# Cross-attention on one core: whole-batch stacks in three buffers, fewer transfers, one exponential per pair of heads

## The chip, the core and the metric

One core of a Trainium2 chip. The metric is the device time of one execution in microseconds; the profile shows one such execution, with the work of TensorE (PE, its weight loads PEld), VectorE (DVE), ScalarE (ACT), GpSimd (POOL) and the transfers, which nearly all are issued by SyncE's queue (SP).

## The reference

Sixteen batches of 256 queries of width 320 attend to 256 keys with 20 heads of 16. The last 8 keys of each batch are special: 4 "dummy" and 4 "ip" keys, which have a softmax of their own and a mask from bounding boxes.

```python
B, S, D = hidden_states.shape                      # 16, 256, 320
text = encoder_hidden_states[:, :end_pos]          # 248 keys of width 512
ip_h = encoder_hidden_states[:, end_pos:]          # 8 keys
q = _split_heads(hidden_states @ w_q, 20)
k, v = _split_heads(text @ w_k, 20), _split_heads(text @ w_v, 20)
out_text = _merge_heads(_sdpa(q, k, v))            # softmax(q k' / 4) v
mask_ip = _ip_mask(bbox, B, S, dtype)
k_ip, v_ip = _split_heads(ip_h @ w_k_ip, 20), _split_heads(ip_h @ w_v_ip, 20)
out_ip = _merge_heads(_sdpa(q, k_ip, v_ip, mask=mask_ip))
out = (out_text + out_ip) @ w_out + b_out + hidden_states
```

## The kernel before

Two stages follow each other; each engine has one instruction stream, written out by hand, with semaphores between them.

**Projections.** Eight groups of two batches (`group(g)` on each engine). PE forms ten tiles: three of K, four of V, three of Q. A float32 product is made of three matmuls with operands split in a high and a low part. ACT copies the high part of a K or Q tile out of PSUM, DVE forms the low part (L533), and SP stores both (L204, L209) in `q_parts` and `k_parts` in DRAM; V goes to `v_rows` (L242). Each part of a buffer is written again only when its store has landed. In the last group the query scores and maxima of batch 0 are interleaved (`FIRST_SCORES`), and SP issues the first stack loads there (`first_loads`).

**Batches.** Every batch has ten pairs of heads. For each of the two heads of a pair a *stack* of rows is built in SBUF: three groups of 16 rows (high, low, high of Q against high, high, low of K), five mask rows, and two rows that carry the negated row maxima. One matmul over 55 rows then gives a score that is already masked and has its maximum taken off. `q_stack` and `k_stack` have two buffers (batch parity `u`), and each is loaded in two halves of five pairs: `load_stack_q` is 6 transfers of parts (L286) and 2 of masks (L289), `load_stack_k` is 6 (L300).

In batch b the engines do, per pair p:
- PE: `key_scores(b, p)` (L728, keys in partitions, into `score_t`), which waits for both exponentials of the pair before it, and at p = 0 and 5 for the rows of maxima of that half; in even pairs `values` of two finished pairs (L745 into `pv`); `query_scores(b + 1, p)` (L675, into `score_q`, 53 rows, which at p = 0 and 5 waits for the stack of the next batch and always for the maxima of two pairs before); in odd pairs `project_out` for batch b - 1 (L755 into `pj`).
- ACT: two exponentials of 512 columns (L477) and, in even pairs, the evacuation of `pv` (L468), behind the exponentials of that pair.
- DVE: `maxima(b + 1, p)` (L542 and L544); in odd pairs `invert` (L598 transposes 32 x 32 blocks, L601 takes reciprocals); `turn_back` (L606) at p = 8 for its own batch and at p = 2 and 4 for the one before, which waits for POOL's sums; `finish` (L613, adds the residual) at p = 0 and 6; at p = 4 and 9 `turn` (L552), which turns the maxima of a half into rows.
- POOL, `normalise(b)`: waits for the residual x of the batch, adds the bias to it (L386), then for each of five blocks scales (L392) and adds (L397).
- SP, `batch(b, u)`: rows of half 1 of b stored (`store_rows`, four transfers, L214), Q half 1 of b + 1, rows of half 1 loaded (`load_rows`, L222, which waits for the store to land), K half 1 of b + 1, output of b - 2 (L343), residual of b (L309), values of b + 1 (L304, L306), rows of half 0 of b + 1 stored, Q half 0 of b + 2 once half of batch b's key scores are done, rows of half 0 loaded, K half 0 of b + 2.

Batches 0, 1, 14 and 15 are written out, 2 to 13 run in a loop of two batches a turn.

## Time and profile before

| | |
|---|---|
| three runs | 658.9, 652.2, 658.66 us; median 658.66 |
| the profiled run's own time | 657.42 us |
| span of its profile | 655.6 us |
| busy: PE, DVE, ACT, POOL | 523.5, 387.5, 297.8, 125.7 us |
| mean granted TensorE clock | 0.911 |
| moved by DMA | 107.36 MB, 164 GB/s over the span |

A span is the time from the first to the last instruction. Engines run side by side, so busy times don't add up, and an engine's idle time costs something only where the work behind it sets the end. A line of the timeline gives start, length, engine and source line, operation, output and inputs, and in brackets how long the engine was idle before it and what ended that. Neighbouring instructions of a kind are merged (x4).

### The profile page before, as it was taken

The numbers are of one execution on the slowest core, as the hardware profiler recorded it, in microseconds if no ns is written. First come the engines' busy times: TensorE is split into PE (matmuls) and PEld (weight loads), VectorE is DVE, ScalarE is ACT, GpSimd is POOL, SyncE is SP. The second block draws the span as 40 slices with busy tenths as digits, with TensorE's granted clock in tenths as the row PEclk, the third lists the DMA queues.
The fourth block names the chain that finished last, engine by engine and source line by source line (L and its number), as shares of the span: only waits on it lengthen the run. The fifth ranks groups of instructions, "written<-read, shape, count | busy, mean of one in ns | idle before, by whom it ended". The sixth has DMA issues, their size and how long they took to land.

```text
span 655.6 us, 13734 instructions
## 1 busy us (share of the span) xinstructions
PE 523.5 (80%) x4304; PEld 337.8 (52%) x4304; DVE 387.5 (59%) x706; ACT 297.8 (45%) x515; POOL 125.7 (19%) x203
## 2 busy tenths in 40 slices
PE   4969899999977667866878678787787877878686
PEld 3868778887855344433434344343443434434342
DVE  2565443435335476847568576685766857668543
ACT  4442443434411454535446364464644646446372
POOL 4040000000000032121322213222132221322232
PEclk9979899999978587979899798898989979889899
DMA  9987888888786645353453624526445363452411
GB/s 270 289 243 166 296 266 287 266 274 283 253 208 164 148 132 152 79 171 83 143 155 86 181 76 144 162 74 171 103 133 156 86 171 94 135 160 77 129 46 40
DMA packets 96808, 107.36 MB, mean 164 GB/s; under 512 B 20988, under 2 KB 75836, under 8 KB 96784
## 3 DMA queue, kind: packets, MB, share of 16 engines
q1 hardware_dynamic: 96032, 105.99, 55.2%
q0 software_dynamic: 752, 1.07, 1.3%
q8 instruction: 13, 0.21, 0.1%
q14 instruction: 11, 0.09, 0.0%
HBM read 68.85 MB, written 38.17 MB: 163 GB/s over the span
## 4 chain that ended last, share of the span: by engine, by line
PE 38%; SPq 22%; issue 13%; DMA 12%; DVE 10%; POOL 2%; ACT 1%; DVEq 1%; POOLq 0%; ACTq 0%
PE pv L745 9%; DMA k_stack<-k_parts 7%; SPq L286 6%; PE pj L755 5%; SPq L300 5%; SPq L214 5%; PE score_q L675 4%; DVE max_cols L542 3%; PE score_t L728 3%; DMA probs<-in_wv_ip 2%; PE score_t L636 2%; PE score_t L637 2%; PE score_t L638 2%; DMA v_rows<-v_out 2%; SPq L289 2%
## 5 line engine op out<-in xcount | busy, mean ns | idle before, releaser
L542 DVE TENSOR_REDUCE max_cols<-score_q 128x4 fp32r<-128x992 f32 x160 | 189.1, 1182 | 142.3 <-PE score_q L675 140.2
L477 ACT ACTIVATE probs<-score_t 128x512 f32<-128x512 f32 x320 | 173.7, 595 | 161.2 <-PE score_t L728 159.6
L745 PE MATMUL pv<-probs,v_cur 128*32 128x256 f32 x1920 | 140.3, 432 | 0.7 <-ACT probs L477 0.6
L675 PE MATMUL score_q<-k_stack,q_stack 53*128 53x256 f32 x640 | 80.6, 332 | 45.8 <-DMA k_stack<-k_parts 40.0
L728 PE MATMUL score_t<-q_stack,k_stack 55*128 55x256 f32 x640 | 79.3, 328 | 36.9 <-ACT probs L477 20.2
L755 PE MATMUL pj<-wo_sb,o_all 128*128 128x320 f32 x192 | 78.8, 510 | 29.0 <-DVE out_sb L613 18.7
L675 PEld LDWEIGHTS score_q<-k_stack,q_stack 53*128 53x128 f32 x640 | 53.4, 204 | 87.9 <-issue 57.3
L728 PEld LDWEIGHTS score_t<-q_stack,k_stack 55*128 55x128 f32 x640 | 52.5, 200 | 76.9 <-issue 42.2
L745 PEld LDWEIGHTS pv<-probs,v_cur 128*32 128x32 f32 x1920 | 59.6, 121 | 50.2 <-issue 19.5
L386 POOL TENSOR_TENSOR x_all<-x_all,bias_sb 128x640 f32<-128x640 f32 x16 | 24.7, 1544 | 305.1 <-DMA x_all<-in_x 305.1
L392 POOL TENSOR_TENSOR o_turned<-o_turned,inv_cols 128x256 f32<-128x256 f32 x80 | 49.6, 620 | 167.4 <-DVE inv_cols L601 167.4
L468 ACT ACTIVATE o_all<-pv 128x512 f32<-128x512 f32 x80 | 47.9, 598 | 53.9 <-PE pv L745 53.9
L598 DVE STREAM_TRANSPOSE o_turned<-o_all 128x512 f32<-128x512 f32 x80 | 55.9, 698 | 11.2 <-ACT o_all L468 11.2
L755 PEld LDWEIGHTS pj<-wo_sb,o_all 128*128 128x128 f32 x192 | 32.0, 201 | 50.8 <-DVE out_sb L613 22.0
L521 DVE TENSOR_TENSOR c_hl<-o_all,c_hl 128x1024 fp32r<-128x1024 f32 x16 | 19.0, 1223 | 54.2 <-ACT c_hl L411 54.2
L397 POOL TENSOR_TENSOR o_all<-o_turned 128x128 f32<-128x128 f32 x80 | 36.4, 456 | 10.1 <-POOL o_turned L392 6.7
L544 DVE TENSOR_REDUCE max_cols<-score_q 128x4 fp32r<-128x32 f32 x160 | 29.0, 181 | 0.0
L422 ACT ACTIVATE qk_out<-score_t 128x512 fp32r<-128x512 f32 (+1 forms) x24 | 14.0, 593 | 27.7 <-PE score_t L638 16.3
L636 PE MATMUL pj<-c_hl,wk_hl 128*128 128x512 f32 x32 | 14.3, 446 | 11.3 <-DVE c_hl L521 11.3
L533 DVE TENSOR_TENSOR qk_out<-score_t,qk_out 128x512 fp32r<-128x512 f32 (+1 forms) x24 | 15.8, 683 | 11.8 <-ACT qk_out L422 11.8
L601 DVE RECIPROCAL inv_cols<-o_turned 128x16 f32<-128x16 f32 x80 | 20.3, 254 | 2.7
L606 DVE STREAM_TRANSPOSE o_all<-o_all 128x256 f32<-128x256 f32 x48 | 20.7, 431 | 1.0 <-POOL o_all L397 1.0
(128 smaller groups left out, 644.8 us busy)
## 6 DMA issues: line engine op xcount, KB each, us to landing
q_stack<-q_parts SPq DMA_DIRECT2D x192, 80.0 KB
k_stack<-k_parts SPq DMA_DIRECT2D x192, 80.0 KB
v_rows<-v_out SPq DMA_DIRECT2D x32, 320.0 KB, 2.4
v_cur<-v_rows SPq DMA_DIRECT2D x16, 640.0 KB
o_all<-in_ctxT SPq DMA_DIRECT2D x16, 512.0 KB, 5.7
q_parts<-qk_out SPq DMA_DIRECT2D x32, 256.0 KB, 2.4
k_parts<-qk_out SPq DMA_DIRECT2D x32, 248.0 KB, 4.4
x_all<-in_x SPq DMA_DIRECT2D x16, 320.0 KB, 3.3
```

The source lines that it names most:

```text
L214: sp.dma_start(max_rows[h].rearrange("r (t i n) -> i r t n", t=2, i=4)[i], row_buf[32 * i:32 * i + 32, h, :].rearrange("r (t n) -> r t n", ...
L286: sp.dma_start(qv[at:at + DH, :, :], src).then_inc(done, 16)
L392: pool.tensor_tensor(out, out, inv_cols[:, k, :].unsqueeze(2).broadcast_to([P, 2 * S // 32, DH]), ALU.mult).then_inc(scaled, 1)
L397: pool.tensor_tensor(o_norm_t[:, k // 2, :, half:half + DH], out[:, 0:S // 32, :], out[:, S // 32:, :], ALU.add).then_inc(o_added, 1)
L468: nc.scalar.activation(o_raw[:, k, :], pv[:, :], ACT.Copy)\
L477: nc.scalar.activation(probs[:, slot(u, p), 2 * S * e:2 * S * (e + 1)], score_t[:, 512 * e:512 * e + 512], ACT.Exp, scale=SCALE)\
L542: nc.vector.tensor_reduce(out=max_cols[:, h, :, at:at + 2].rearrange("p t e -> p e t"), in_=both[:, :, :, 0:TEXT], op=ALU.max, axis=AX.X, ...
L598: nc.vector.transpose(turned_blocks(k), o_raw[:, k, :].rearrange("p (j n) -> p j n", n=32))\
L675: last = mm(score_bank(first, p, e)[:, t * KEYS:(t + 1) * KEYS], q_cols(u, p, e, PART + MASKS, t * P, P), k_cols(u, p, e, PART + MASKS, 0, ...
L728: last = mm(score_t[:, 512 * e + S * tile:512 * e + S * tile + S], k_cols(u, p, e, PART + MASKS + 2, tile * P, P), q_cols(u, p, e, PART + ...
L745: last = mm(pv[32 * t:32 * t + 32, at:at + S], values_of(u, kind, 4 * k + t), probs[:, slot(u, 2 * k + t // 2), a:a + S], start=kind != 1, ...
L755: last = mm(pj[:, 0:D], o_norm[:, u, c, t * P:t * P + P], wo_sb[:, c, :], start=c == 0, stop=c == OC - 1)
```

## The change

Stacks are loaded whole, two batches ahead, into three buffers in turn (`w`, the batch's number modulo 3; `r` counts a buffer's uses). The third lies in `stack2`, where the split context of the projections (`c_hi`, `c_lo`) lies before. `q_parts` is laid out by head, high then low part, so that 32 rows (high and low) of a head come in one transfer: 6 for Q and masks, 6 for K. Two transfers load the constant mask rows of the third buffer (`load_kaux`). SP's order per batch is new. The rows of maxima of a half are stored in one transfer. ACT has one exponential of 1024 columns per pair, and waits once for key scores. PE does query scores ahead of values. The loop body now holds six batches and turns twice.

```diff
-    q_parts = nc.dram_tensor("q_parts", [2, D, B * S], f32, kind="Internal").ap()
+    q_parts = nc.dram_tensor("q_parts", [H, 2, DH, B * S], f32, kind="Internal").ap()
...
+        stack2 = sb("stack2", [P, PAIRS * (S + KEYS)], f32r)
+        c_hi = stack2[:, 0:CC * GT].rearrange("p (c n) -> p c n", c=CC)
+        c_lo = stack2[:, CC * GT:2 * CC * GT].rearrange("p (c n) -> p c n", c=CC)
+        q_stacks = [q_stack[:, 0, :], q_stack[:, 1, :], stack2[:, 0:PAIRS * S]]
+        k_stacks = [k_stack[:, 0, :], k_stack[:, 1, :], stack2[:, PAIRS * S:PAIRS * (S + KEYS)]]
...
+            for c in range(2):
+                body(Turn(0, c))
+            with eng.Fori(0, 2) as i:
+                for c in range(2, 8):
+                    body(Turn(i, c))
+            for c in (B - 2, B - 1):
+                body(Turn(0, c))
...
-                        sp.dma_start(q_parts[s, m * P:m * P + r, bass.ds(g * GT, GT)], src[:, s, :])\
+                        sp.dma_start(q_parts[8 * m:8 * m + r // DH, s, :, bass.ds(g * GT, GT)], src[:, s, :])\
...
             def store_rows(b, h):
                 sp.wait_ge(rows_turned, 2 * b + h + 1)
-                for i in range(4):
-                    sp.dma_start(max_rows[h].rearrange("r (t i n) -> i r t n", t=2, i=4)[i],
-                                 row_buf[32 * i:32 * i + 32, h, :].rearrange("r (t n) -> r t n", t=2))\
-                        .then_inc(rows_stored, 16)
+                sp.dma_start(max_rows[h].rearrange("r (t i n) -> i r t n", t=2, i=4),
+                             row_buf[:, h, :].rearrange("p (t n) -> p t n", t=2)).then_inc(rows_stored, 16)
...
             def first_loads():
...
-                load_stack_q(0, 0, 0)
-                load_stack_k(0, 0, 0)
+                load_stack(Turn(0, 0))
+                load_stack(Turn(0, 1))
...
+            def load_stack(t):
+                done = stack_loaded[t.w]
+                qv = q_stacks[t.w].rearrange("p (a n) -> p a n", a=PAIRS).bitcast(f32)
+                kv = k_stacks[t.w].rearrange("p (a n) -> p a n", a=PAIRS).bitcast(f32)
+                q_cols_of = q_parts[:, :, :, bass.ds(t.b * S, S)].rearrange("(a e) s r n -> e (s r) a n", e=2)
+                masks = aux_rows[bass.ds(t.b, 1), :, :].rearrange("a r n -> (a r) n")
                 for e in range(2):
+                    at = HEAD * e
+                    sp.dma_start(qv[at:at + DH, :, :], q_cols_of[e, 0:DH]).then_inc(done, 16)
+                    sp.dma_start(qv[at + DH:at + PART, :, :], q_cols_of[e]).then_inc(done, 16)
+                    sp.dma_start(qv[at + PART:at + PART + MASKS, :, :],
+                                 masks.unsqueeze(1).broadcast_to([MASKS, PAIRS, S])).then_inc(done, 16)
+                for j, part in enumerate((0, 1, 0)):
+                    src = k_parts[part, :, bass.ds(t.b * KEYS, KEYS)].rearrange("(a e r) n -> e r a n", e=2, r=DH)
                     for e in range(2):
                         at = HEAD * e + DH * j
+                        sp.dma_start(kv[at:at + DH, :, :], src[e]).then_inc(done, 16)
...
+            store_rows(0, 1)
+            load_rows(Turn(0, 0), 1)
+            sp.wait_ge(tile_ready, 10 * GROUPS)
+            load_kaux(2)
+            def batch(t):
+                b, u = t.b, t.u
+                if t.there(2):
+                    need(sp, st_ready, PAIRS * b)
+                    load_stack(t.to(2))
+                if t.there(-2):
                     store_out(b - 2)
                 load_residual(b, u)
+                if t.there(1):
                     need(sp, pv_ready, QUADS * b)
                     load_values(b + 1, 1 - u)
+                    for h in range(2):
+                        store_rows(b + 1, h)
+                        load_rows(t.to(1), h)
...
+                    if t.there():
+                        act.wait_ge(st_ready, PAIRS * b + p + 1)
+                        if p % 2 == 0:
+                            need(act, pv_ready, QUADS * b + (p - 4) // 2 + 1)
+                        nc.scalar.activation(probs[:, slot(u, p), :], score_t[:, :], ACT.Exp, scale=SCALE)\
+                            .then_inc(exp_done, 1)
...
                 for p in range(PAIRS):
+                    if t.there():
+                        key_scores(t, p)
+                        if t.there(1):
+                            query_scores(t.to(1), p)
                     for k, off in VALUES.get(p, ()):
+                        if t.there(off):
                             values(b + off, (u + off) % 2, k)
-                    if there(b) and there(b, 1):
-                        query_scores(b + 1, 1 - u, p)
```

## Rows read from the trace of the kernel before

**Rows 1.** The page, part 4: chain that ended last, shares of the span.
```profile
PE 38%; SPq 22%; issue 13%; DMA 12%; DVE 10%; POOL 2%; ACT 1%; DVEq 1%; POOLq 0%; ACTq 0%
```

**Rows 2.** Timeline of PE: first key scores of the first and last batch.
```profile
213.10 0.40 PE L728 MATMUL score_t<-q_stack,k_stack 55*128 55x256 f32 x4
...
625.84 0.51 PE L728 MATMUL score_t<-q_stack,k_stack 55*128 55x256 f32 x4 [0.29 <-ACT probs L477]
```

**Rows 3.** Timeline of PE in one batch: key and query scores.
```profile
406.44 0.50 PE L728 MATMUL score_t<-q_stack,k_stack 55*128 55x256 f32 x4 [0.20 <-ACT probs L477]
...
410.22 0.50 PE L728 MATMUL score_t<-q_stack,k_stack 55*128 55x256 f32 x4 [0.93 <-ACT probs L477]
...
412.42 0.40 PE L728 MATMUL score_t<-q_stack,k_stack 55*128 55x256 f32 x4
412.66 0.40 PE L675 MATMUL score_q<-k_stack,q_stack 53*128 53x256 f32 x4
...
415.06 0.50 PE L728 MATMUL score_t<-q_stack,k_stack 55*128 55x256 f32 x4
...
418.72 0.50 PE L728 MATMUL score_t<-q_stack,k_stack 55*128 55x256 f32 x4 [1.29 <-DMA q_stack<-max_rows]
421.24 0.80 PE L675 MATMUL score_q<-k_stack,q_stack 53*128 53x256 f32 x4 [2.02 <-DMA k_stack<-k_parts]
...
423.33 0.79 PE L728 MATMUL score_t<-q_stack,k_stack 55*128 55x256 f32 x4
...
427.03 0.40 PE L728 MATMUL score_t<-q_stack,k_stack 55*128 55x256 f32 x4
...
430.25 0.51 PE L728 MATMUL score_t<-q_stack,k_stack 55*128 55x256 f32 x4
```

**Rows 4.** Timeline of ACT: a pair's two exponentials, and one alone.
```profile
412.86 1.08 ACT L477 ACTIVATE probs<-score_t 128x512 f32<-128x512 f32 x2
...
415.59 0.60 ACT L477 ACTIVATE probs<-score_t 128x512 f32<-128x512 f32 x1 [1.65 <-PE score_t L728]
```

**Rows 5.** Stretches: length, busy us, granted clock, DMA share of 16 engines, GB/s.
```profile
406.40:434.00 27.60, 21.34 (x212) 11.68 (x212) 18.86 (x38) 13.76 (x25) 6.83 (x11) 0.88 0.45 127
406.40:418.70 12.30, 9.53 (x116) 5.37 (x116) 11.07 (x23) 7.19 (x13) 2.15 (x4) 1.00 0.27 74
418.70:426.90 8.20, 6.16 (x40) 3.01 (x42) 2.70 (x7) 2.17 (x4) 3.61 (x5) 0.58 0.78 224
...
107.10:127.90 20.80, 20.80 (x109) 17.18 (x108) 8.22 (x10) 8.62 (x14) 0.00 (x0) 1.00 0.85 281
...
180.30:183.40 3.10, 3.10 (x18) 2.29 (x17) 1.55 (x3) 0.61 (x2) 0.00 (x0) 1.00 0.78 151
...
632.70:633.40 0.70, 0.70 (x6) 0.30 (x4) 0.67 (x3) 0.35 (x1) 0.00 (x0) 1.00 0.10 33
```

**Rows 6.** Timeline of SP's queue in the same batch: issues, their length and count.
```profile
408.91 2.49 SPq L214 DMA_DIRECT2D max_rows<-row_buf  x4
...
415.32 0.54 SPq L222 DMA_DIRECT2D q_stack<-max_rows  x2
415.96 2.67 SPq L300 DMA_DIRECT2D k_stack<-k_parts  x6
...
419.43 0.39 SPq L309 DMA_DIRECT2D x_all<-in_x  x1
```

**Rows 7.** The page, part 6: row stores, KB each, median us to landing.
```profile
max_rows<-row_buf SPq DMA_DIRECT2D x128, 8.0 KB, 2.3
```

**Rows 8.** Timeline of POOL in the same batch.
```profile
422.90 1.54 POOL L386 TENSOR_TENSOR x_all<-x_all,bias_sb 128x640 f32<-128x640 f32 x1 [8.94 <-DMA x_all<-in_x]
...
426.31 0.46 POOL L397 TENSOR_TENSOR o_all<-o_turned 128x128 f32<-128x128 f32 x1
```

**Rows 9.** Timeline of DVE: a block's inversion, maxima, and a transpose back.
```profile
411.67 0.70 DVE L598 STREAM_TRANSPOSE o_turned<-o_all 128x512 f32<-128x512 f32 x1
...
412.63 1.19 DVE L542 TENSOR_REDUCE max_cols<-score_q 128x4 fp32r<-128x992 f32 x1
...
413.83 0.43 DVE L606 STREAM_TRANSPOSE o_all<-o_all 128x256 f32<-128x256 f32 x1
```

More of the change, by code:

```diff
@@ L236, in group @@
                 store_qk(g, 2)
-                if not more:
-                    load_stack_q(0, 0, 1)
                 for t in range(2 * GB):
@@ L243, in group @@
                         .then_inc(v_stored[t % 2], 16)
-                    if t == 1 and not more:
-                        load_stack_k(0, 0, 1)
                 if more:
@@ L672, in query_scores @@
                     need(pe, max_done, n if first else n - 1)
[L673 removed]
+                for tile in range(2):
                     for e in range(2):
[L675 to L677 removed]
+                        last = mm(score_bank(first, p, e)[:, tile * KEYS:(tile + 1) * KEYS],
+                                  q_cols(w, p, e, PART + MASKS, tile * P, P),
+                                  k_cols(w, p, e, PART + MASKS, 0, KEYS), start=True, stop=True)
                 last.then_inc(sq_ready, 1)
```

160 lines of the change are left out of this document (56 added, 104 removed).

## The prediction

> **What bounds the kernel now.** I read the page first, then the starts of the key-score matmuls (L728) in TensorE's timeline, then one batch of it against the other engines' timelines, then SP's queue, and last the stretches with their DMA share.
>
> No engine is the bound by itself: in the chain that ended last PE holds 38%, SP's queue 22%, DMA 12%, DVE 10% [rows 1]. So the stages have to be taken apart. The first key scores start at 213.10 us and those of the last batch at 625.84 us [rows 2]: 15 batches lie between, 27.52 us each. Ahead of them stand 213 us of projections, behind them 29.8 us of last batch and tail.
>
> One batch, from 406.44 us and 27.6 long [rows 3, 5], taken apart by the starts of L728 [rows 3]. The undisturbed rhythm is two pairs of heads in 3.78 us (406.44 to 410.22): key scores, values, the evacuation, the next exponentials, key scores; of these the even pair has 2.20 and the odd pair 1.58 (410.22 to 412.42 is 2.20). Five such make 18.9. Above it stand: 1.06 us where L755 waits for DVE's L606 (412.42 to 415.06 is 2.64 instead of 1.58); 1.46 us for the maxima rows (415.06 to 418.72 is 3.66 instead of 2.20); 3.03 us for the K stack and what follows at half clock (418.72 to 423.33 is 4.61 instead of 1.58); 1.50 us of half clock (423.33 to 427.03 is 3.70 instead of 2.20); and 1.64 us where L755 waits for DVE's L613 (427.03 to 430.25 is 3.22 instead of 1.58). The sum is 27.59, the batch's length. 5.99 us of it come from the transfers of SP and from the clock that falls in their wait: the stretch 418.7 to 426.9 was granted 0.58, the one before it 1.00 [rows 5]. 2.70 us come from DVE being late.
>
> Why the K stack is late: SP spends 2.49 us on the four stores of L214, then 3.9 on the Q half and its gaps, and only then issues the row loads (415.32) and the K half (415.96 to 418.6) [rows 6]. It can't start earlier, since with two buffers the first half is freed in mid-batch.
>
> **The change part by part.**
>
> *Three buffers, two batches ahead.* A stack that is loaded a whole batch before its query scores can't be waited for: the K wait and the half clock go. The rows of the second half are stored and loaded straight after their transpose, about 9 us ahead of pair 5: that wait goes too. That is the 5.99 us. What is next is a closed ring, which I work out, because the order on SP is new: rows of half 1, then 12 stack transfers, then output, residual, values, then rows of half 0.
>
> Ring A starts as DVE ends transpose L552 of half 1. Store: one issue, 0.6 us (one of the four took that), at most 2.5 (all four), I take 0.6; it lands 2.3 us later [rows 7]; row loads 0.54 [rows 6]; 3.5 us to the first stack issue. The 12 stack issues cost SP about 0.45 each (2.67 for six in L300) and 0.28 to 0.37 for the masks [rows 6], 5.4 in all; more than 0.45 for twice the bytes isn't indicated, since L309 with 320 KB takes 0.39. But the data do not follow so fast: 1.92 MB of parts, 0.10 of masks, 0.33 of output and 0.33 of residual are 2.68 MB, and at full share the transfers before moved 287 GB/s (224 at 0.78) [rows 5]: 9.3 us, 10.7 at 250, and with 1.5 for the first byte and the landing 11.5 from the first stack issue. Then POOL: L386 at 422.90 to the second L397's end at 426.77 are 3.9 us [rows 8]. DVE needs these two blocks for L606 at pair 8 (0.43 us), and stands in it with the rest of the batch behind it: maxima of pair 9 (1.20), L598 and L601 (0.96) [rows 9]; 2.6, and I leave 0.2 for the small L552 and the semaphores. 3.5 + 11.5 + 3.9 + 2.8 = 21.7 us per batch. In the kernel before, this residual is issued at 419.43 [rows 6], 13 us into the batch, and has 11 more until pair 8 (430.25) [rows 3]: covered. Now the cover is gone.
>
> *Query scores ahead of values.* In even pairs they move between key scores and values. That delays the values, the evacuation and the next exponential by 0.24 us (two interleaved groups start 0.23 to 0.24 apart: 412.42, 412.66) [rows 3]. *One exponential per pair:* two of 512 columns end 1.08 us after the first one's start, though one takes 0.60 [rows 4]: they overlap, and the second adds 0.48. If 512 columns cost that, 1024 need 0.96 to 1.08; and where the exponential waited for key scores it now starts one matmul (0.1) later. I take nothing, from -0.1 to +0.1 a pair. The cycle is 3.78 + 0.24 = 4.02, five of them 20.1. DVE gets the scores of even pairs 1.4 us earlier and has 18.9 us of work in a batch [rows 5], under these 20.1, so both waits for it (2.70) should go. Ring A with 21.7 is longer, so the period is 21.7 us. Bounds: 20.1 if the residual comes as before (3.5 us after its issue at 6.3: ring 20.0), 23.5 if the transfers run at 250 GB/s (22 with them alone) and the clock falls again in some batches.
>
> *Rows of half 0* are stored behind the values in the same queue: 3.34 MB (the values are 0.66) from the first stack issue are 11.6 to 13.4 us, then 1.5 to store, 0.54 and 1.8 to load: 18.9 to 20.7 after the ring's start. The next batch's first key scores are due 1.2 to 3 us before the ring closes, at 18.7 to 20.5. A wait of up to 2 us; as it closes only over two batches (20.7 + 20.1 + 1.2 = 42.0) it doesn't set the period by itself. It lies in the range.
>
> *The start.* The first loads are two whole stacks, 24 issues (11 us) instead of 12 (5.4), in front of L209's stores. Twice the bytes before the first query scores and stores 5 us later: 0 to 7, I take 4. Loading the mask rows of the third buffer: two issues, hidden behind batch 0.
>
> *The store of the Q parts.* The destination's outermost dimension is now 8 heads (4 for the last tile) instead of 128 (64) rows. What a narrow outer dimension does is seen in the row loads, two partitions each: in a stretch in which hardly anything else moved, 33 GB/s at a DMA share of 0.10 of 16 engines, under two engines' worth (the last row of [rows 5]). If the stores spread over 8 and 4 engines, the first four engines take more. A group of 20.8 us has 640 such packets of 2 KB (rows of 512), 40 an engine; now 16 from each of six stores, 96. At 281 GB/s and share 0.85 a packet takes 0.1 us, so 56 of them add 5.6 to the 17.7 (0.85 of 20.8) an engine has [rows 5]: 23.3 against PE's 20.8. Bounds 0 and 2.5 us a group over 7 groups, 0 to 17; I take 10, as packets get cheaper where the other engines idle.
>
> The Trainium skill ("DMA: Bandwidth & Descriptors", on why a DMA increments its semaphore by 16) states that a transfer runs on the largest number of engines up to 16 that divides the slowest dimension of both sides; by that rule it is 8 and 4 here, and the sum would have 17 in place of 10. The trace agrees for the two-row loads alone.
>
> **The sum.** 655.6 - 15 x (27.52 - 21.7) = 655.6 - 87.3; + 4 at the start; + 10 in the projections: 582.3 us of span. The profiled run's own time is 657.4, the median of the three runs 658.7, 3.1 above the span: 585 us.
>
> **The rivals.**
> *The clock stays the trouble* (24 us): the period is over 23.5, because waits of 2 us at the batch's start (rows of half 0) or at pair 8 let the clock fall, as 418.72 to 421.24 did. For it: the wait of 2.02 at 421.24 was followed by half clock [rows 3, 5]. Against: the stretch before it holds waits of 1.06 and 1.46 and was granted 1.00. 655.6 - 53 + 14 + 3 = 620.
> *No ring at all* (20.1), no narrow stores: 655.6 - 111 + 4 + 3 = 552. For it: 3.5 us from the residual's issue (419.43) to L386 (422.90) before [rows 6, 8]. Against: 2 MB never stood in front of it.
> *The narrow stores bind fully and the start costs 7:* 655.6 - 87.3 + 17 + 7 + 3 = 595; if landings of the V rows come late too, up to 605.
> *Slower:* the big stack loads don't reach the rate. In 180.3 to 183.4 us, with stack transfers issued, only 151 GB/s moved at a share of 0.78 [rows 5]. With 151 the 2.68 MB take 17.7 us, ring A 29.9, and the kernel comes to 655.6 + 36 + 14 + 3 = 709. It decides from a period of 26.6, at 185 GB/s. Against it: SP issued only 1 MB there in 6 us, so the rate was not asked for, and in mid-kernel 287 at full share.
> *The change doesn't do what it says:* a wait for a stack remains, because loads start after the rows' trip: they land 14 of 21.7 us into the batch, 7 us early. I give it nothing of its own.
>
> **How the numbers follow.** Ring A as forecast (570 to 592): 0.36. Ring A with narrow stores that bind fully (592 to 605): 0.24. Clock trouble (605 to 645): 0.17. No ring (below 570): 0.14. Rate falls short partly, period 25 to 27 (645 to 665): 0.04. Slower: 0.05. The range 560 to 622 takes the first two wholly, most of the no-ring case and half of the clock's: 0.8. A measurement of this kernel can tell about 1% from no change, that is 6.6 us. Faster by over 1%: 0.92; within 1%: 0.03; slower: 0.05.
>
> **What would show it.** Period of the L728 starts 21 to 22.5 us. No wait of L675 for k_stack. In DVE's waits L606 for POOL's L397, about 1 to 2 us a batch at pair 8: that is the ring; if it isn't there and the period is 20, the no-ring case. L386 waits for x until some 15 us into the batch. In the projections a group over 20.8 with waits of ACT or DVE on DMA shows the narrow stores. The prediction is wrong if the granted clock in the batches stays at 0.9, or if L728 waits for max_rows at each batch's start.

## The result, and the profile after

| kernel | time, us (median) | ratio to the kernel before, 95% interval |
|---|---|---|
| before, run beside it | 655.84 | |
| after | 749.1 (738.89 to 749.38) | 1.139 (1.126 to 1.151) |

The change makes the kernel 14% slower; the forecast was 585 us. Of the runs below only the second of n_early (683.4 us, 1.5% above its first) fell in a slower state, and comparisons go by the first. The profiled execution took 749.25 us with a span of 747.5, and its mean granted clock fell from 0.911 to 0.85.

The page, part 4, shares of the span in the chain that ended last, by engine and by line. It answers to [rows 1].

```profile
DMA 37%; SPq 22%; PE 15%; issue 13%; DVE 7%; ACT 3%; POOL 3%; ACTq 0%; DVEq 0%; POOLq 0%
DMA out<-out_sb 20%; SPq L292 5%; DMA q_parts<-qk_out 5%; PE pv L725 5%; DMA max_rows<-row_buf 5%; PE pj L734 5%; DMA v_rows<-v_out 4%; SPq L214 4%; SPq L219 3%; PE score_t L711 2%; SPq L286 2%; SPq L284 2%; DMA probs<-in_wv_ip 2%; SPq L285 2%; DVE qk_out L520 2%
```

PE fell from 38% to 15%, transfers rose from 12% to 37%, and more than half of that is one kind of transfer, the output of a batch (L334, `store_out`). Line numbers have moved: L711 is now `key_scores`, L661 `query_scores`, L734 `project_out`, L725 `values`, L596 `finish`, L537 `turn`, L284 to L292 the stack loads, L223 and L229 the rows of maxima.

The waits of the kernel after: total us, times, longest.

```profile
POOL x_all L376 <- DMA x_all<-in_x: 460.7, 16, 226.3
PE pj L734 <- DVE out_sb L596: 108.8, 13, 10.5
DVE out_sb L596 <- DMA out<-out_sb: 108.1, 12, 10.5
ACT qk_out L412 <- DMA q_parts<-qk_out: 58.5, 16, 6.4
PE score_q L661 <- DMA k_stack<-k_parts: 21.0, 1, 21.0
```

TensorE's timeline: the last group's first projection (this line alone from the kernel before, then from the kernel after), the first query scores, and the first key scores of the first and of the last batch (the last two answer to [rows 2]).

```profile
173.93 0.40 PE L636 MATMUL pj<-c_hl,wk_hl 128*128 128x512 f32 x1
```
```profile
191.08 0.47 PE L620 MATMUL pj<-stack,wk_hl 128*128 128x512 f32 x1 [1.48 <-DVE stack L508]
...
222.42 0.80 PE L661 MATMUL score_q<-k_stack,q_stack 53*128 53x256 f32 x4 [20.96 <-DMA k_stack<-k_parts]
...
252.04 0.40 PE L711 MATMUL score_t<-q_stack,k_stack 55*128 55x256 f32 x4
...
715.70 0.50 PE L711 MATMUL score_t<-q_stack,k_stack 55*128 55x256 f32 x4 [0.32 <-ACT probs L466]
```

The batches begin at 252.04 instead of 213.10, 38.9 us late. Fifteen periods take 463.7 us, 30.91 each instead of 27.52: another 50.9. From the last batch's start to the end of the span are 31.8 us instead of 29.8, 2.0 more. The three parts are the 91.9 us by which the spans differ (747.5 - 655.6), but for rounding.

One batch on SP's queue (issues, their length and count). It answers to [rows 6].

```profile
416.95 0.34 SPq L284 DMA_DIRECT2D q_stack<-q_parts  x1
...
422.55 0.43 SPq L334 DMA_DIRECT2D out<-out_sb  x1
423.17 0.39 SPq L305 DMA_DIRECT2D x_all<-in_x  x1
...
427.21 0.56 SPq L223 DMA_DIRECT2D max_rows<-row_buf  x1
439.01 0.56 SPq L229 DMA_DIRECT2D q_stack<-max_rows  x2
445.12 0.55 SPq L223 DMA_DIRECT2D max_rows<-row_buf  x1
447.98 0.53 SPq L229 DMA_DIRECT2D q_stack<-max_rows  x2
448.79 0.34 SPq L284 DMA_DIRECT2D stack<-q_parts  x1
```

DVE and POOL in the same batch:

```profile
435.71 0.49 DVE L596 TENSOR_TENSOR out_sb<-pj,x_all 128x320 f32<-128x320 f32 x1 [9.16 <-DMA out<-out_sb]
...
444.90 0.18 DVE L537 STREAM_TRANSPOSE row_buf<-max_cols 128x64 f32<-128x64 f32 x1
```
```profile
436.58 1.54 POOL L376 TENSOR_TENSOR x_all<-x_all,bias_sb 128x640 f32<-128x640 f32 x1 [17.71 <-DMA x_all<-in_x]
```

This is the period. The stack loads start at 416.95. The output of batch b - 2, issued behind them at 422.55, has landed only at 435.71, 18.8 us after the first stack issue; until then DVE can't write `out_sb`, of which there is one, and stands 9.16 us in `finish`. The maxima of pair 7 and all that follows stand behind it, and PE waits in L734 for a free `pj`. The rest of the batch takes DVE 9.4 us, up to the rows of half 1, which SP stores at 445.12. They land, their loads are issued at 447.98, and the next stack starts at 448.79: 18.8 + 9.4 + 2.9 + 0.8 = 31.8 us, this batch's period. The residual lands at 436.58, 13.4 us after its issue; before, it took 3.5 [rows 6, 8]. The rows of half 0 are issued at 427.21, and their loads, which wait for the landing, 11.8 us later.

Stretches of the kernel after (length, busy us by engine, granted clock, DMA share, GB/s), beside [rows 5]: all batches, the time in which the burst lands, and the time after it.

```profile
252.00:715.70 463.70, 309.11 (x3148) 177.72 (x3145) 279.31 (x547) 190.18 (x224) 99.84 (x161) 0.82 0.65 112
...
417.50:432.00 14.50, 9.25 (x114) 5.32 (x106) 8.62 (x18) 6.94 (x9) 1.08 (x2) 0.97 1.09 143
435.00:446.00 11.00, 9.42 (x80) 5.17 (x80) 7.38 (x14) 3.56 (x4) 5.49 (x9) 0.71 0.16 56
```

While the burst lands, all 16 engines are full (share 1.09) and move 143 GB/s, where the forecast had 287. After PE's wait of 9.2 us the clock is granted at 0.71, a mixture of the two levels, so part of the work behind the wait also runs slower: the 24 matmuls of `values` take 2.24 us at 439.84 and 1.50 at 444.49.

### The profile page after: what moved, and what is told of

It is laid out like the page before. It is cut to its first block, busy times and chain, and to the rows that moved or that the text cites. A ratio compares the mean times of both kernels' runs of the same rounds, so it can differ in the third digit from the quotient of the medians.

```text
span 747.5 us, 12726 instructions
## 1 busy us (share of the span) xinstructions
PE 526.0 (70%) x4304; PEld 345.3 (46%) x4304; DVE 386.3 (52%) x706; ACT 278.2 (37%) x355; POOL 126.2 (17%) x203
## 4 chain that ended last, share of the span: by engine, by line
DMA 37%; SPq 22%; PE 15%; issue 13%; DVE 7%; ACT 3%; POOL 3%; ACTq 0%; DVEq 0%; POOLq 0%
DMA out<-out_sb 20%; SPq L292 5%; DMA q_parts<-qk_out 5%; PE pv L725 5%; DMA max_rows<-row_buf 5%; PE pj L734 5%; DMA v_rows<-v_out 4%; SPq L214 4%; SPq L219 3%; PE score_t L711 2%; SPq L286 2%; SPq L284 2%; DMA probs<-in_wv_ip 2%; SPq L285 2%; DVE qk_out L520 2%
## 5 line engine op out<-in xcount | busy, mean ns | idle before, releaser
L466 ACT ACTIVATE probs<-score_t 128x1024 f32<-128x1024 f32 x160 | 163.4, 1021 | 204.9 <-PE score_t L711 204.6
L734 PE MATMUL pj<-wo_sb,o_all 128*128 128x320 f32 x192 | 85.9, 566 | 110.9 <-DVE out_sb L596 108.8
L725 PE MATMUL pv<-probs,v_cur 128*32 128x256 f32 x1920 | 136.1, 422 | 1.5 <-DMA v_cur<-v_sp_rows 1.0
L734 PEld LDWEIGHTS pj<-wo_sb,o_all 128*128 128x128 f32 x192 | 38.7, 231 | 131.0 <-DVE out_sb L596 112.8
L725 PEld LDWEIGHTS pv<-probs,v_cur 128*32 128x32 f32 x1920 | 58.4, 119 | 49.7 <-issue 17.4
L711 PE MATMUL score_t<-q_stack,k_stack 55*128 55x256 f32 x440 | 59.7, 351 | 30.0 <-ACT probs L466 19.1
L596 DVE TENSOR_TENSOR out_sb<-pj,x_all 128x320 f32<-128x320 f32 x32 | 15.4, 481 | 113.3 <-DMA out<-out_sb 108.1
L711 PEld LDWEIGHTS score_t<-q_stack,k_stack 55*128 55x128 f32 x440 | 36.4, 203 | 79.9 <-issue 34.5
L661 PE MATMUL score_q<-k_stack,q_stack 53*128 53x256 f32 x440 | 50.5, 310 | 31.6 <-DMA k_stack<-k_parts 21.0
L661 PEld LDWEIGHTS score_q<-k_stack,q_stack 53*128 53x128 f32 x440 | 38.9, 212 | 35.2 <-DMA k_stack<-k_parts 21.2
L508 DVE TENSOR_TENSOR stack<-o_all,stack 128x1024 fp32r<-128x1024 f32 x16 | 19.0, 1222 | 58.1 <-ACT stack L401 58.1
L711 PE MATMUL score_t<-stack 55*128 55x256 f32 x200 | 27.1, 351 | 14.7 <-ACT probs L466 7.9
L711 PEld LDWEIGHTS score_t<-stack 55*128 55x128 f32 x200 | 16.3, 201 | 38.3 <-issue 23.9
L620 PE MATMUL pj<-stack,wk_hl 128*128 128x512 f32 x32 | 15.7, 492 | 25.7 <-DVE stack L508 25.7
```

Source lines behind the costliest of these rows:

```text
L466: nc.scalar.activation(probs[:, slot(u, p), :], score_t[:, :], ACT.Exp, scale=SCALE)\
L661: last = mm(score_bank(first, p, e)[:, tile * KEYS:(tile + 1) * KEYS], q_cols(w, p, e, PART + MASKS, tile * P, P), k_cols(w, p, e, PART + ...
L711: last = mm(score_t[:, 512 * e + S * tile:512 * e + S * tile + S], k_cols(t.w, p, e, PART + MASKS + 2, tile * P, P), q_cols(t.w, p, e, PAR ...
L725: last = mm(pv[32 * t:32 * t + 32, at:at + S], values_of(u, kind, 4 * k + t), probs[:, slot(u, 2 * k + t // 2), a:a + S], start=kind != 1, ...
L734: last = mm(pj[:, 0:D], o_norm[:, u, c, t * P:t * P + P], wo_sb[:, c, :], start=c == 0, stop=c == OC - 1)
```

## The experiments

All ratios are to the kernel before, run beside each. The theory to begin with: transfers that others wait for (output, residual, rows of maxima) stand in one queue behind a burst of stack loads that moves slowly. It has rivals for each half: the layout in DRAM, the addresses, the amount in one burst, SP's issues.

**The output and the residual ahead of the stacks** (a_early):

```diff
+                if t.there(-2):
+                    store_out(b - 2)
+                load_residual(b, u)
                 if t.there(2):
                     need(sp, st_ready, PAIRS * b)
                     load_stack(t.to(2))
-                if t.there(-2):
-                    store_out(b - 2)
-                load_residual(b, u)
```

> The changed kernel with one edit: in SP's order per batch, the output of b - 2 and the residual of b stand ahead of the 12 stack transfers instead of behind them. Theory 1 (the ring): the period of 31.5 us is set by the output that lands 13 us after its issue, behind the stack, and holds DVE's L596 and all behind it; ahead of the stack it lands in 3 us, the waits of L596 for it (108 us in all) go, and the period falls to 24 to 27 us, time 650 to 690. Rival (the rate): the stack transfers at 135 GB/s fill 15 us of the batch anyway and the rows of half 0 wait behind them, so the period stays near 31: 740. Projections and first query scores stay as in the changed kernel.

Measured 693.9 us, 1.063 (1.056 to 1.070): 55 us less, with a mean period of 27.2 us, both just above what the theory had (650 to 690, 24 to 27). The waits for the output are gone. What still stands behind the burst now sets the end, the rows of half 0:

```profile
PE score_t L711 <- DMA q_stack<-max_rows: 55.7, 9, 12.9
PE score_t L711 <- DMA stack<-max_rows: 26.1, 5, 6.3
```

So the ring through `out_sb` is shown, but the burst is still slow: from the store of the rows of half 0 to their load it is 13.4 us in a batch read (406.48 to 419.83), beside the 11.8 above.

**The old layout of the Q parts** (a_oldq), with three transfers of 16 rows in place of one of 16 and one of 32, 14 in all:

```diff
-    q_parts = nc.dram_tensor("q_parts", [H, 2, DH, B * S], f32, kind="Internal").ap()
+    q_parts = nc.dram_tensor("q_parts", [2, D, B * S], f32, kind="Internal").ap()
...
-                    sp.dma_start(qv[at:at + DH, :, :], q_cols_of[e, 0:DH]).then_inc(done, 16)
-                    sp.dma_start(qv[at + DH:at + PART, :, :], q_cols_of[e]).then_inc(done, 16)
+                    for j, part in enumerate((0, 0, 1)):
+                        src = q_parts[part, :, bass.ds(t.b * S, S)].rearrange("(a e r) n -> e r a n", e=2, r=DH)[e]
+                        sp.dma_start(qv[at + DH * j:at + DH * (j + 1), :, :], src).then_inc(done, 16)
```

> The changed kernel with q_parts laid out as before (part, row, column), so that the stores of Q parts have 128 or 64 outermost rows again, and the Q loads are 6 transfers of 160 KB instead of 4 of 160 and 320. Theory (narrow stores): a group of the projections returns from 24.2 to 20.9 us, 17 us less by the last group; the batches don't change, 732. Rival (the layout is also what slows the stack loads, with its step of 1 MB between pairs): the 1 KB packets of the Q part take 46 ns again and the period falls by 5 us or more: under 670. Second rival: the slower projections have another cause, and nothing changes there: 749.

Measured 749.2 us, 1.148 (1.133 to 1.163): no gain. TensorE's timeline of this kernel has the last group's first projection 19.9 us earlier than the kernel after (191.08):

```profile
171.19 0.40 PE L620 MATMUL pj<-stack,wk_hl 128*128 128x512 f32 x1
```

All of that is lost in the batches, whose mean period rises from 30.9 to 32.3 us, 21 us over fifteen. The narrow stores cost about 20 us; with the output behind the burst, the 32-row loads that they allow save about as much. With the output ahead of it they don't: the period is 27.2 us with the new layout (a_early) and 27.4 with the old (n_early, below), and the old layout is 21 us faster in all.

**Other addresses in DRAM** (a_pad): each row of `q_parts` and `k_parts` is 4 KB longer.

```diff
-    k_parts = nc.dram_tensor("k_parts", [2, D, B * KEYS], f32, kind="Internal").ap()
+    k_parts = nc.dram_tensor("k_parts", [2, D, B * KEYS + 1024], f32, kind="Internal").ap()[:, :, 0:B * KEYS]
```

> The changed kernel with every row of q_parts and k_parts 4 KB longer in DRAM, all else equal. Theory (addresses): many 1 KB reads whose addresses lie at powers of two apart (16 KB, 512 KB, 1 MB) collide; with the longer rows they spread, packets take about 50 ns instead of 130, the stack lands in 8 us instead of 16, the period falls to 24 us or less, 640. Rival (the target): the rate is bound where 16 or 32 partitions are written, and the period stays 31.5: 749.

Measured 744.8 us, 1.141 (1.122 to 1.161), within the interval of the kernel after. The theory had 640: the distance of the rows is not the cause.

**The burst spread over the batch** (a_spread): the kernel a_early, but the 12 transfers go out one or two per pair of heads, behind a wait for that pair's key scores.

> The kernel of a_early with the 12 stack transfers not issued in a row but one or two after each pair's key scores, so that one or two are in flight. Theory (backlog): a stack transfer is only slow when many are queued; spread out its packets take 46 ns as in the kernel before, nothing waits behind them, the period falls to 20 to 22 us, 585 to 610. Rival (the rate is low whatever the spacing, 135 GB/s): the 2 MB need 15 us of the batch and small transfers behind them wait some us each; period 24 or more, over 640.

Measured 714.2 us, 1.094 (1.080 to 1.109), slower than a_early. PE waits less for the rows of maxima (18.5 us instead of 81.8), but 96.9 us for K stacks, which SP now issues late, since it stands in waits with its queue behind it. The 585 to 610 of the theory did not come; the time is on the rival's side, but as SP's waits alone could make it, the run says nothing on the rate.

**Both reversals together** (n_early = a_early and a_oldq) and **that with every stack transfer cut in two** (n_half, 28 issues of 80 KB instead of 14 of 160):

```diff
-                        src = q_parts[part, :, bass.ds(t.b * S, S)].rearrange("(a e r) n -> e r a n", e=2, r=DH)[e]
+                        src = q_parts[part, 32 * h * n:32 * (h + 1) * n, bass.ds(t.b * S, S)].rearrange(
```

> The changed kernel with both known faults taken away: q_parts stored as before (wide stores, 14 transfers a stack), and output and residual ahead of the stack. Theory: projections at 20.9 us a group, and a period set by the rows of half 0, which wait behind a stack that lands at 125 to 135 GB/s: 27 to 29 us, time 655 to 685. Rival: with the wide stores gone the period falls too: under 640.

> n_early with each stack transfer cut in two (pairs 0 to 4, pairs 5 to 9): 28 issues of 80 KB in a row, the same bytes. Theory (pacing): SP takes 0.45 us an issue, so 80 KB an issue ask for only 178 GB/s, no backlog forms, packets of 1 KB take 46 ns as in the kernel before, and the stack lands in 12.5 us: the period is no longer than in n_early, perhaps 1 to 2 us shorter. Rival (16 rows at a time move at 125 GB/s whatever is asked): packets at 120 ns or more again and the stack takes 16 us.

Measured 673.1 us (1.03, one run, so without an interval; the median with the slower run is 678.3) and 646.0 us, 0.989 (0.984 to 0.994). The same bytes in twice the issues are 27 us faster, with a mean period of 26.0 us instead of 27.4. **The second halves behind the rows of half 0** (n_split):

> n_half with the second half of the stack issued only after the rows of half 0 have been stored and loaded. Theory: nothing urgent waits behind a stack any more; the K wait, the rows wait and the half clock of the kernel before are gone, and the period falls to 21 to 23.5 us, time 565 to 600. Rival (the transfers themselves are the limit, 3.5 MB a batch): period over 25, time over 620.

Measured 662.3 us, 1.015 (1.011 to 1.018), a miss for the theory (565 to 600) and slower than n_half: SP waits out each round trip of the rows and issues the rest late, so PE waits for K stacks again, 80.7 us in all.

**The cut alone in the kernel after** (a_half):

> The changed kernel with one thing undone: each of the 12 transfers of a stack is cut into two of half the pairs (24 issues), order and layout are the changed kernel's. Theory A (a 160 KB transfer in a backlog moves 1 KB in 82 to 225 ns, an 80 KB one in about 46 ns, as in the kernel with the old layout and the output first, where the cut gave 678 to 646 us): the output and the residual land some 2 us a batch earlier, 749 to 700-720 us. Rival B (the bytes in front of the output are what counts, and 12 more issues cost SP 5.4 us): 745 us or more.

Measured 711.9 us, 1.084 (1.076 to 1.091): as expected, 37 us of the 93 lost come back by nothing but smaller transfers. The order is as it was, and PE still waits 86.2 us for `out_sb`.

**What each form of transfer reaches alone** (probe, a kernel of transfers only, executed once):

> A kernel that leaves out the whole computation and only moves data on SP's queue, in steps of which each waits until the one before has landed, so that each transfer form has a rate of its own: (0) 12 loads of 160 KB into 16 partitions in 1 KB pieces, all issued at once, as the changed kernel does; (1) 24 loads of 80 KB of the same bytes, as before; (2) the 12 loads of 160 KB with at most two on their way; (3) 6 loads of 320 KB into 32 partitions; (4) 6 loads of 320 KB into 128 partitions; (5) 6 stores of 256 KB with 128 rows outermost, (6) the same with 8 heads outermost, (7) 6 stores of 128 KB with 4 heads outermost. Theory A (the form itself is slow in a backlog): step 0 runs at about 130 GB/s, 15 us, step 1 at 175, the pace of its issues. Rival B (the form is not slow, the slow rate of the changed kernel comes from what else runs on the chip beside it): step 0 runs at 280 GB/s or more, 7 us or less. For the stores, theory C (they spread over 16, 8 and 4 engines): step 6 at about half of step 5's rate, step 7 at a quarter; rival D (their form is not what counts): equal rates.

Its stretches, in the order of the steps 0 to 7 (length; busy us of DVE and POOL, which are nothing; clock; DMA share; GB/s):

```profile
14.00:23.00 9.00, 0.00 (x0) 0.00 (x0) 1.00 1.16 118
29.00:37.00 8.00, 0.00 (x0) 0.00 (x0) 1.00 1.18 136
43.00:62.00 19.00, 0.00 (x0) 0.00 (x0) 1.00 0.39 90
68.00:73.00 5.00, 0.00 (x0) 0.00 (x0) 1.00 1.12 217
77.00:82.00 5.00, 0.00 (x0) 0.00 (x0) 1.00 1.01 350
85.00:88.00 3.00, 0.00 (x0) 0.00 (x0) 1.00 1.03 381
91.00:98.00 7.00, 0.00 (x0) 0.00 (x0) 1.00 0.50 176
102.00:108.00 6.00, 0.00 (x0) 0.00 (x0) 1.00 0.26 88
```

Loads into 16 partitions move 118 GB/s with every engine full, and in halves 136, where theory A had 175; into 32 partitions 217, into 128 partitions 350. The form is slow by itself. The two rates are enough for the kernel's: 1.31 MB at 118 GB/s and 0.66 MB at 217 are 14 us, an estimate of 140 GB/s, beside the 143 read in the burst. For the stores theory C holds in full: 128 rows outermost 381 GB/s at a share of 1.03, 8 heads 176 at 0.50, 4 heads 88 at 0.26.

**Is it the source or the destination?** (probe2, transfers only, executed once)

> A second kernel that leaves out the whole computation and only moves data, 1.97 MB in 12 transfers of 160 KB in each of the steps 0 to 5, to find what makes the transfer of 16 rows slow (118 GB/s, 154 ns for 1 KB). (0) The form of the stack loads again: 118 GB/s. (1) The same 16 partitions and pieces, but the source is one stretch of 160 KB: if the far apart source addresses are the cause, 250 GB/s and more; if the destination is, 118 again. (2) The source as in 0, but the 16 rows spread over all 128 partitions, every eighth: if it is the 16 neighbouring partitions that all engines write to at once, 250 GB/s and more; if the source, 118. (3) As 0, but only into partitions 0 to 47: if the two halves of the partitions share the load, slower than 0; if one neighbourhood of 16 is what counts, equal. (4) 160 KB into 128 partitions in pieces of 1.25 KB: 300 GB/s if the number of partitions is what counts, not the size of a transfer. (5) The form of 0 as a store: no theory has a number for it. (6) Six transfers of the form of 0, one at a time: the time of one alone.

Its stretches, steps 0 to 5:

```profile
14.00:23.00 9.00, 0.00 (x0) 0.00 (x0) 1.00 1.15 113
28.00:37.00 9.00, 0.00 (x0) 0.00 (x0) 1.00 1.01 140
45.00:51.00 6.00, 0.00 (x0) 0.00 (x0) 1.00 1.12 206
58.00:70.00 12.00, 0.00 (x0) 0.00 (x0) 1.00 1.16 108
75.00:81.00 6.00, 0.00 (x0) 0.00 (x0) 1.00 0.93 282
85.00:92.00 7.00, 0.00 (x0) 0.00 (x0) 1.00 0.85 190
```

One contiguous source instead of scattered rows brings 140 for 113. The same scattered source into every eighth partition brings 206. Partitions 0 to 47 alone (step 3) take 108, about as much as step 0. The 160 KB into 128 partitions move 282, where the pace of SP's issues, 12 in 5.6 us, allows at most 350. So it is mainly neither the size of a transfer (136 for 118 when halved) nor its source, it is which partitions its rows go to. The Trainium skill ("SBUF — State Buffer", Door 1: The DMA port swizzle) states a rule for this: bandwidth depends on how many of 16 ports the partitions reach, a port is chosen by bits 2 to 4 and 6 of the partition number, at some 27 GB/s a port. Neighbours 0 to 15 reach 4 ports (109 GB/s by the page, 104 in its own measurement), 32 neighbours or every eighth of 128 reach 8 (218). The 118, 217 and 206 here agree within 9%, the 118 lying above the page's 109. Step 5 does not come out of the same rule: stores from 16 neighbouring partitions move 190 GB/s, so the limit is shown here for loads only. By the rule every third of 48 partitions reaches 8 ports too.

**The rule tried in the kernel** (n_inter): n_early with the 16 rows of a transfer on every third partition of the head's 48, nothing else changed.

```diff
-                        sp.dma_start(qv[at + DH * j:at + DH * (j + 1), :, :], src).then_inc(done, 16)
+                        sp.dma_start(qv[at + j:at + PART:3, :, :], src).then_inc(done, 16)
```

> The kernel with the old layout of the Q parts and the output and the residual ahead of the stacks (678 us), with one thing changed: the 16 rows of a stack transfer go to every third partition of a head's 48 (part j into rows j, j+3, ...) instead of 16 neighbouring ones; the sums of the scores run over the same rows in another order. Alone on the chip, 16 rows on neighbouring partitions moved at 118 GB/s, the same on every eighth partition at 206. Theory A (the neighbouring partitions of the destination are the limit in the kernel too): the 1.92 MB of a batch take some 9 to 10 us instead of 15, the rows of half 0 behind them land 5 us earlier, and the period falls from 27.4 to 22 to 24 us: 600 to 640 us. Rival B (every third partition is still one neighbourhood, or SP's queue is the bound): 665 us or more.

Measured 626.9 us, 0.961 (0.955 to 0.967), 46 us less than n_early. The first 10 us of a burst, in n_early and then in n_inter (columns as above, with the five engines):

```profile
400.00:410.00 10.00, 9.42 (x88) 5.27 (x90) 8.13 (x18) 5.07 (x6) 3.67 (x5) 0.82 1.13 152
```
```profile
430.00:440.00 10.00, 9.69 (x102) 5.18 (x104) 7.97 (x18) 5.59 (x7) 3.70 (x5) 0.84 1.00 181
```

SP's queue of n_early, where the store of the rows behind the burst is issued and where their load could be:

```profile
408.31 0.57 SPq L223 DMA_DIRECT2D max_rows<-row_buf  x1
421.33 0.56 SPq L229 DMA_DIRECT2D q_stack<-max_rows  x2
```

and the same in n_inter:

```profile
439.48 0.61 SPq L223 DMA_DIRECT2D max_rows<-row_buf  x1
446.20 0.56 SPq L229 DMA_DIRECT2D q_stack<-max_rows  x2
```

13.0 us have become 6.7. Part of that is SP, which issues this burst more slowly; from the burst's first issue to the load of the rows it is 22.9 us (398.39 to 421.33) and 18.4 (427.83 to 446.20). The mean period falls from 27.4 to 24.9 us, not quite to the 22 to 24 expected, and the start takes 7.7 us less. The neighbouring partitions made the burst slow in the kernel itself. The price is SP's: six such K transfers take it 3.96 us to issue (as in c_inter's line below), where six with neighbouring partitions took 2.67 [rows 6].

**The three small parts**, all on the kernel before (b_all3) and each alone (b_rows, b_first, b_exp):

```diff
-                for i in range(4):
-                    sp.dma_start(max_rows[h].rearrange("r (t i n) -> i r t n", t=2, i=4)[i],
+                sp.dma_start(max_rows[h].rearrange("r (t i n) -> i r t n", t=2, i=4),
...
+                    if there(b) and there(b, 1):
+                        query_scores(b + 1, 1 - u, p)
                     for k, off in VALUES.get(p, ()):
...
+                        nc.scalar.activation(probs[:, slot(u, p), :], score_t[:, :], ACT.Exp, scale=SCALE)\
```

> The kernel before with the three small parts of the change alone: row maxima stored in one transfer, one exponential per pair, query scores ahead of values. Two buffers, halves and the layout stay. Theory: SP gains 1.9 us per half and with it the rows and K waits shrink by that much, the two waits of PE for DVE (2.7 us a batch) shrink: 20 to 60 us faster, 595 to 635. Rival: the K stack is freed late and sets the period by itself: within 1%.

> The kernel before with one part of the change alone: the row maxima of a half go to DRAM in one transfer instead of four; everything else is as before. In the kernel with all three small parts the time fell from 653 to 583 us. Theory A (the store carries it): SP spends some 1.9 us less per half in front of the second Q half, the row loads and the K half, so the wait for the rows (1.46 us in the batch read) and the stall of the K stack with its half clock (4.5 us) shrink or go: up to 5 us a batch, 75 us, and at least 40: 580 to 612 us. Rival B (DVE's lateness carries it, so that this part alone is worth little): the K half is still waited for, 640 to 655 us.

> The kernel before with one part alone: in even pairs TensorE computes the next batch's query scores ahead of the values instead of behind them. Theory A: the two waits for DVE of a batch (1.06 and 1.64 us at L755) go, at 0.24 us for each of five even pairs: 2.7 less 1.2 is 1.5 us a batch, 22 us: about 630 us. Rival B: DVE only waits in another place, and each pair pays the 0.24 us: 15 x 1.2 is 18 us more, 671 us. Rival C: the batch is set by SP's transfers, so nothing changes: 650 to 660 us.

> The kernel before with one part alone: one exponential of 1024 columns per pair of heads instead of two of 512. Two of them ended 1.08 us after the first one's start, and the one of 1024 takes 1.02 us in the changed kernel, but it starts only when the second key score is there. Theory A (worth nothing): 648 to 660 us. Rival B (one operation less for each of 160 pairs, and the evacuations of ScalarE come earlier): 0.1 us and more a pair, 16 us and more: below 640 us. Rival C (the later start costs 0.1 to 0.2 us a pair): 670 to 685 us.

| kernel | time, us | ratio (95%) |
|---|---|---|
| b_all3 | 582.9 | 0.889 (0.885 to 0.893) |
| b_rows | 603.6 | 0.922 (0.916 to 0.927) |
| b_first | 623.2 | 0.951 (0.946 to 0.957) |
| b_exp | 654.5 | 1.000 (0.997 to 1.003) |

b_all3 is faster than the 595 to 635 expected; the other three lie in or near their theory's range.

Waits of the kernel before:

```profile
PE score_q L675 <- DMA k_stack<-k_parts: 40.0, 18, 3.6
PE pj L755 <- DVE out_sb L613: 18.7, 15, 1.3
PE score_t L728 <- DMA q_stack<-max_rows: 16.7, 14, 2.2
PE pj L755 <- DVE o_all L606: 10.4, 16, 1.3
```

of b_rows:

```profile
PE score_q L673 <- DMA k_stack<-k_parts: 30.6, 20, 2.6
...
PE score_t L726 <- DMA q_stack<-max_rows: 2.0, 1, 2.0
```

and of b_first:

```profile
PE pj L755 <- DVE o_all L606: 1.9, 2, 1.3
...
PE pj L755 <- DVE out_sb L613: 0.6, 1, 0.6
```

One store instead of four takes 24 us out of PE's waits for transfers, and with them some of the clock's falls (mean clock 0.911 to 0.958): 52 us in all. Query scores ahead of values take 27 us out of PE's waits for DVE, and 32 out of the time. The exponential is worth nothing: one of 1024 columns takes 1.02 us, two overlapping ones of 512 took 1.08 [rows 4].

**The loop of six batches** (b_loop6), b_all3 with the changed kernel's loop form:

```diff
-            with eng.Fori(1, B // 2 - 1) as i:
-                for u in range(2):
-                    body(2 * i + u, u)
+            with eng.Fori(0, 2) as i:
+                for c in range(2, 8):
+                    body(6 * i + c, c % 2)
```

> The kernel with the three small parts (583 us) in the loop form of the changed kernel: a body of six batches that turns twice, instead of two batches that turn six times; order, buffers and transfers stay. Theory A (the longer body has to be fetched: TensorE's waits for nothing shown were up to 7 us in the changed kernel): 3 to 7 us for each turn and engine start, 590 to 600 us. Rival B (fetching runs ahead and is hidden): 580 to 586 us.

Measured 598.6 us, 0.915 (0.907 to 0.922): 16 us slower than b_all3, as theory A had it. But its period is longer all along (23.6 us instead of 22.8), not at two turns, so where the fetching would hurt is not shown.

**Three buffers in the old order** (c_best): half transfers, old layout, SP's order of the kernel before with each load one batch earlier, and the small parts. **c_inter** adds the interleaving of n_inter.

> A kernel put together from what the runs showed: three stack buffers and loads two batches ahead as in the changed kernel, but in half transfers of 80 KB, with the parts laid out in DRAM as before, in SP's order of the kernel before (the output and the residual between the halves), and the three small parts. The kernel with the three small parts and two buffers alone ran at 583 us with a period of 22.5 us (21.5 and 25 in turn). Theory A (what is left of the wait for the stacks goes, TensorE and ScalarE set the pace): a period of 20.1 to 21.5 us, 550 to 570 us. Rival B (SP's queue, with its 28 issues and two waits for rows, or fetching the instructions of a loop body of six batches is the bound): a period of 22.5 us or more, 583 us and above.

> The kernel with three buffers, half transfers in short bursts and the small parts (577 us), with the same interleaving of the rows over partitions. Its bursts are 6 to 8 transfers of 80 KB and run at 46 ns for 1 KB in the stretch read. Theory A (short bursts do not run into the limit): nothing, 570 to 583 us. Rival B (some bursts do): 560 us or less.

Measured 576.8 us, 0.883 (0.877 to 0.888), and 634.5 us, 0.972 (0.966 to 0.979). c_best is the fastest kernel here, but slower than its theory (550 to 570) and only 1% below b_all3, and their intervals overlap: its mean period is 22.1 us for the 22.8 of b_all3, and the six-batch loop is in it. c_inter is a miss for both theories. SP's queue in c_best, then in c_inter with its chain by engine:

```profile
404.43 2.67 SPq L303 DMA_DIRECT2D k_stack<-k_parts  x6
```
```profile
405.87 3.96 SPq L303 DMA_DIRECT2D k_stack<-k_parts  x6
```
```profile
SPq 48%; PE 21%; issue 14%; DMA 8%; DVE 5%; POOL 3%; ACT 1%; POOLq 0%; DVEq 0%; ACTq 0%
```

With 28 issues a batch, 0.21 us more for each of the 24 loads of parts are 5 us a batch. The mean period rises from 22.1 to 25.9 us, and SP is nearly half of the chain, where c_best has it at 19%. Where a burst was the bound the interleaving paid; where SP's issues are, it costs.

## Why the prediction was wrong

- *"... at full share the transfers before moved 287 GB/s (224 at 0.78) [rows 5]: 9.3 us, 10.7 at 250, and with 1.5 for the first byte and the landing 11.5 from the first stack issue."* This step failed. The 287 GB/s of [rows 5] were read in a stretch that also moved output, residual and values, over 128 partitions; 1.92 of the 2.68 MB go to 16 or 32 neighbouring partitions, which take 118 or 217 GB/s (probe). The doubled size of the transfers is a second part: cut in two, they give 37 us back (a_half). From the first stack issue to the output's landing it took 18.8 us. The prediction even had the mark in hand: 151 GB/s at a share of 0.78 [rows 5], that is 194 at full share, and explained it by SP's issue rate. The right rate was the slower rival's, given 0.05: with 151 GB/s it had a period of 29.9, and the measured one is 30.9. By its own terms that period is 29.4 (3.5 + 17.7 + 1.5 + 6.7), so the closeness is in part luck: the burst took 18.8 us to the output, and the ring closed in another place. The Trainium skill's section on the port swizzle, cited above, would have given that rival far more; it was overlooked.
- *Ring A closes through the residual, POOL and L606 at pair 8 (3.9 + 2.8).* The ring exists, but closes earlier, through the output: `finish` at pair 6 needs `out_sb` free. The prediction listed the output's bytes, not who waits for its landing. Behind it stand 9.4 us of DVE's batch instead of 6.7. So the ring of 3.5 + 11.5 + 6.7 = 21.7 is really 3.67 + 18.76 + 9.41 = 31.84 in the batch read: 7.3 us from the rate and 2.7 from the place.
- *Rows of half 0 behind 3.34 MB: a wait of up to 2 us.* With the output out of the way (a_early) they are the next bound, with 12.9 us as the longest wait. Same cause, the rate.
- *The start: 0 to 7, taken as 4.* First key scores came 38.9 us late. The last group begins 17 us later than before (191.08 against 173.93), with the narrow stores. The rest, about 22, is the start: from there to the first key scores it is 61.0 us instead of 39.2, and PE waited 20.96 us for the first stack, before 2.88. Of the 57.0 us of n_early the interleaving of n_inter takes 7.7, so the rate is a part; the rest comes with the two whole stacks in front, and how it divides is not shown.
- *Narrow stores: 10, bounds 0 to 17.* Measured 17.2 up to the last group's start against the kernel before, and 19.9 against a_oldq. The mechanism was right and its full price was due, at or above the upper bound; the Trainium skill's rule, which the prediction named and had as 17, was the better guide (0.50 and 0.26 of the engines, as it says of 8 and 4).
- *The cycle without the ring, 20.1 us a batch,* was right: the last period of the kernel after, in which no stack is loaded any more, is 19.7 us long (695.96 to 715.70), while those before it are 28 to 34.
- *"No wait of L675 for k_stack"* held in the batches: the wait went, and PE waited for the rows of maxima only twice (10.8 and 6.9 us). More than the 5.99 us of [rows 3] was given back by what the same burst did to the transfers behind it.
- *One exponential: nothing.* Right (b_exp). *DVE's two waits go for 0.24 us in every even pair.* Right (b_first), worth 32 us.
- *The single row store* was folded into the three buffers' gain and never priced by itself. Alone it is worth 52 us, more than any other part.

What stays open: which part of the six-batch loop costs 16 us; and why the pace of 80 KB transfers in short bursts doesn't fall to the 136 GB/s that a long burst of them reaches. That a short run drains before the ports fill is only argued. Nor do the runs say why stores from 16 neighbouring partitions don't show the limit of the loads.

## What to carry to other kernels

Before transfers are merged or moved into one burst, work out the burst's rate from the partitions that each one reaches, not from a mean over a stretch, and then list every transfer behind it in the queue with the one who waits for its landing: here 6 us a batch of waits saved became 9 us of waits made, through a single output buffer. Cost each part of a bundle by itself, since the cheapest one, four stores made into one, held the largest gain and the headline part the loss. Look first at what SP must issue between a store and the load that depends on it.

## What the runs showed of the hardware

- Loads into 16 neighbouring partitions, in a backlog with 16 busy engines, move 108 to 118 GB/s in transfers of 160 KB, 136 in transfers of 80 KB and 140 from a contiguous source; into every eighth partition 206, into 32 neighbours 217, into 128 partitions 350 (probe, probe2). Stores from 16 neighbours moved 190. A share of 1.1 of the DMA engines says nothing of the bytes.
- A store whose outermost dimension is 8 runs at 176 GB/s and a share of 0.50, one of 4 at 88 and 0.26, against 381 at 1.03 with 128 rows.
- A transfer to every third partition takes SP 0.66 us to issue instead of 0.45.
- Under a backlog the wait of a small transfer is that of the queue: in the batch read 32 KB of row maxima landed 11.8 us after their issue, 320 KB of residual 13.4; the latter took 3.5 before.
- Rows in DRAM 4 KB further apart changed nothing measurable (a_pad).
